# Linear attention: the second half of the scores goes from PSUM to SBUF by ScalarE and is masked there by GpSimd

## The chip, the cores and the metric

The kernel is one program on 1 core of one Trainium2 chip. The metric is the device time of one execution in microseconds (us). The profile is of one execution; its times and its rows are on the same core.

## What is computed

A decoder of two layers over x (64 batches of 128 tokens by 128 channels, f32): linear attention, cross attention, a local transformer of depth two, a Mamba block, cross attention to the context, and a mixture of experts. The change touches the first of these, linear attention with 16 heads of 8 channels, for each batch:

```
q, k, v = split(layernorm(x) @ Wqkv + bqkv)           # heads of 8
feat(t) = exp(clip(unit(t) @ omega * sqrt(2s) - s, -20, 20)) * weight   # 64 features a head
scores  = feat(k) @ feat(q)^T, with zero where the key is later than the query
out     = (scores^T @ v) / max(scores^T @ 1, 1e-6)
x       = x + out @ Wout + bout
```

The reference sums the keys up chunk by chunk; masked scores over the 128 tokens give the same. The mask is a triangle of ones and zeros (`g.tri`, 128x128) by which the scores of every head are multiplied.

## The kernel before

`linear_attention` runs the 64 batches through a pipeline of seven places, NORM, QKV, KEY, FEAT, SCORE, OUT and LAST, numbered 0 to 6. Step n of the pipeline works on batch n at NORM, on batch n - 1 at QKV and so on, so one step holds a piece of each of up to seven batches. `pipeline` writes the first 8 steps out, then runs a loop whose body is 4 steps (14 turns), then 8 more steps in which the batches run out. Every engine has its own `step` function, whose order is written by hand, and executes its instructions strictly in that order. Engines wait for one another by counting semaphores: `Stage.at(name, b)` is the count at which an operation on batch b is done, and `ago=1` or `ago=2` means the batch one or two before, used where a buffer has to be free again.

The scores of one batch are computed in two halves of 8 heads, both into the same PSUM tensor `score` (128 x 1024 f32). The second half's matmuls (`scores(b, 1)`, L432) can start only when the first half was read out. The masked scores stand in SBUF as `sm` (128 x 2 x 1024), one buffer for even and one for odd batches.

In one step, in this order:

- **TensorE:** the features `feat` of FEAT (L449); the second half of the scores of SCORE (L432); the product of masked scores and values of OUT (L469); the q, k, v matmul of QKV (L477); the last projection of LAST (L485); the transposes of the attention output `oT` (L492) and of q and k (L501); the first half of the scores of FEAT (L432); the transpose of `att` (L515); and last the transpose of the normed x of NORM, `xn` (L522), which waits for GpSimd.
- **VectorE:** the mask of the first half (L555), the statistics of the norm (L563 to L566), the mask of the second half (L570), two clips of the exponentials (L579), the bias of q, k, v (L587), the residual (L593), the division by the denominator (L599, L601, L604), the sums of squares (L611, L614).
- **ScalarE:** L373 and L375 (the length of q and k), two exponentials (L382), the copy of `oT` out of PSUM (L388), L393 and L395 (`rstd` of the norm), the squares (L399), and the copies `qkT` (L404), `attT` (L409) and `xnT` (L414).
- **GpSimd:** q and k times their inverse length (L335), the values (L339), then for NORM x minus its mean (L346), that times `rstd` (L350, gives `xn`) and x plus bias (L352).
- **SyncE** loads x.

A matmul group that waits holds up what stands behind it on TensorE. The three waits of interest are those of L469 (`vec_mask1`, the second mask of its batch), of the first half of the scores (`vec_mask1` of the batch before, which frees `score`) and of L522 (`pool_norm`).

Of the kernel before, what the change touches and what calls it, by code (L numbers as in the profile page):

```python
# [13 lines left out]
T = 128  # L14
# [210 lines left out]
def linear_attention(nc, g):  # L225
# [8 lines left out]
    with ExitStack() as stack:  # L234
# [29 lines left out]
        vec_qkv = Stage(m.sem("vec_qkv"), "qkv ss ssm")  # L264
        vec_mask1 = Stage(m.sem("vec_mask1"), "m1")
        vec_feat = Stage(m.sem("vec_feat"), "clip0 clip1")
# [27 lines left out]
        with nc.Block() as block:  # L294
# [19 lines left out]
            def _(gp):  # L314
# [6 lines left out]
                for i in range(4):  # L321
                    gp.memset(by_head(vpad[i])[:, :, :, HD:HD + 1], 1.0).then_inc(zeroed, 1)
                for stage in (pool_norm, pool_key):
                    stage.start(gp)
# [4 lines left out]
                def step(at):  # L329
                    b = at(KEY)  # L330
                    if b:
                        l = b.lane
                        qk = qkv[l][:, 0:2 * C].rearrange("p (h e) -> p h e", e=HD)
                        gp.wait_ge(*act_key.at("rn", b))
                        gp.tensor_tensor(qk, qk, ss[l][:, 2].unsqueeze(2).to_broadcast([T, 2 * H, HD]), ALU.mult  # L335
                                         ).then_inc(*pool_key.did("qkn"))
                        gp.wait_ge(*pe_out.at("pv", b, ago=4))
                        split = lambda ap: ap.rearrange("p (j k e) -> p j k e", k=2, e=HD)
                        gp.tensor_tensor(by_head(vpad[b.slot])[:, :, :, 0:HD], split(qkv[l][:, 2 * C:3 * C]),  # L339
                                         split(g.ones[:]), ALU.mult  # L340
                                         ).then_inc(*pool_key.did("v"))
                    b = at(NORM)
                    if b:
# [14 lines left out]
            def _(sc):  # L358
# [4 lines left out]
                sc.activation(fbias[:, 1:2], fbias[:, 0:1], ACT.Ln).then_inc(prep, 1)  # L363
                for stage in (act_norm, act_turn, act_qkv, act_key, act_keyT, act_feat, act_out, act_att):
                    stage.start(sc)
                sc.wait_ge(prep, 8)

                def step(at):
# [16 lines left out]
                    if b:  # L385
                        sc.wait_ge(*pe_out.at("pv", b))
                        sc.wait_ge(*pe_out.at("pvT", b, ago=2))
                        sc.activation(two(oT[b.lane][:]), feat[:, 0, 0:2 * T], ACT.Copy).then_inc(*act_out.did("oT"))  # L388
                    b = at(NORM)
                    if b:  # L390
# [28 lines left out]
            def _(te):  # L419
# [16 lines left out]
                def step(at):  # L436
# [22 lines left out]
                    if b:  # L459
                        te.wait_ge(*vec_mask1.at("m1", b))  # L460
                        te.wait_ge(*pool_key.at("v", b))
# [42 lines left out]
                    if b:  # L504
                        te.wait_ge(*vec_feat.at("clip0", b))
                        te.wait_ge(*vec_mask1.at("m1", b, ago=1))
                        scores(b, 0).then_inc(*pe_score.did("s0"))
# [19 lines left out]
            def _(v):  # L527
# [16 lines left out]
                mm.then_inc(prep, 1)  # L544
                for stage in (vec_norm, vec_qkv, vec_mask1, vec_feat, vec_mask, vec_out, vec_last):
                    stage.start(v)
# [3 lines left out]
                def step(at):  # L550
# [9 lines left out]
                    if b:  # L560
# [5 lines left out]
                        v.bn_aggr(mv[l][:], stats[l][:]).then_inc(*vec_norm.did("mv"))  # L566
                    b = at(SCORE)
                    if b:
                        v.wait_ge(*pe_score1.at("s1", b))
                        v.tensor_tensor(sm[b.lane][:, 1].rearrange("p a i h t -> p (a i h) t"),  # L570
                                        score[:].rearrange("p a i t -> p (a i) t"),
                                        g.tri[:].unsqueeze(1).to_broadcast([T, 8, T]), ALU.mult
                                        ).then_inc(*vec_mask1.did("m1"))
                    b = at(FEAT)
# [2175 lines left out]
```

## Time and profile before

| what | us |
|---|---|
| median of 3 runs | 4103.48 |
| lowest and highest run | 4102.70, 4106.04 |
| span of the profiled execution | 4103.4 |
| linear attention in it, to the start of the next part | 0 to about 490 |
| TensorE busy, of the whole span | 3856.4 (94%) |
| VectorE busy | 3013.6 (73%) |
| ScalarE busy | 2823.1 (69%) |
| GpSimd busy | 1820.6 (44%) |

The profile gives no time of its own for the execution beside the span; the span lies within the three runs, 0.1 us from their median. PE is TensorE's matmuls, PEld its weight loads, DVE VectorE, ACT ScalarE, POOL GpSimd, SP SyncE. The shares are averages over eight parts of the program with different limits; linear attention is about an eighth of the time.

### The profile page before, as it was taken

How to read it: one execution, taken by the hardware profiler on the slowest of the kernel's cores; microseconds unless marked ns; L12 is line 12 of the kernel's file. 1: busy time of each engine (PE TensorE's matmuls, PEld its weight loads, DVE VectorE, ACT ScalarE, POOL GpSimd, SP SyncE). 2: the span in 40 equal slices, each digit the busy share in tenths (PEclk: the TensorE clock that was granted, in tenths of full speed). 3: DMA queues.
4: the chain of work that ended last, by engine and by line, in shares of the span. 5: the costliest groups of instructions: out<-in, count | busy, mean ns of one | idle time of the engine just before them, and what ended most of it. 6: DMA issues, size and time to landing. Idle time of an engine off the chain costs nothing. (4 is left out here: it accounts for less than half of the span.)

```text
span 4103.4 us, 106549 instructions
## 1 busy us (share of the span) xinstructions
PE 3856.4 (94%) x33992; PEld 2993.1 (73%) x33992; DVE 3013.6 (73%) x7587; ACT 2823.1 (69%) x6420; POOL 1820.6 (44%) x1728
## 2 busy tenths in 40 slices
PE   7888899999979999898999989999999989998999
PEld 5666688888746666685666677888888867776777
DVE  7888655555569999657999955777777767775665
ACT  5666455555569999757999975777777767774333
POOL 3333222222258888536777753333333321112443
PEclk9999999999999999999999999999999989999999
DMA  0000100000010000100000010000000000000000
GB/s 18 9 9 10 48 8 6 6 6 6 7 43 9 8 8 8 27 18 10 8 8 8 13 28 29 1 0 0 0 0 0 0 3 4 3 3 6 12 12 12
DMA packets 109259, 42.48 MB, mean 10 GB/s; under 512 B 91232, under 2 KB 107872, under 8 KB 108512
## 3 DMA queue, kind: packets, MB, share of 16 engines
q1 hardware_dynamic: 109152, 41.10, 3.9%
q8 instruction: 61, 1.00, 0.1%
q14 instruction: 46, 0.38, 0.0%
HBM read 20.16 MB, written 4.19 MB: 6 GB/s over the span
## 5 line engine op out<-in xcount | busy, mean ns | idle before, releaser
L1142 POOL TENSOR_TENSOR l_rc<-l_rc,l_rs 128x1024 f32<-128x1024 f32 x128 | 303.6, 2372 | 201.4 <-DVE l_rs L1334 201.4
L1209 ACT ACTIVATE l_prob<-l_prob,l_mx 128x128 f32<-128x128 f32 x1024 | 312.1, 390 | 0.0
L1820 POOL TENSOR_TENSOR mb_steps<-w_upto,mb_dta 128x1024 f32<-128x1024 f32 x64 | 121.4, 1896 | 354.7 <-DVE mb_dta L2077 354.7
L711 POOL TENSOR_TENSOR ca_prob<-ca_prob,ca_sm 128x1232 f32<-128x1232 f32 x64 | 143.9, 2249 | 299.3 <-DVE ca_sm L877 299.3
L1234 PE MATMUL l_qk_ps<-w_local,l_hT 128*128 128x512 f32 x512 | 248.8, 609 | 13.1 <-DVE l_rs L1334 11.1
L1136 POOL TENSOR_TENSOR l_prob<-l_prob,l_sm 128x1024 f32<-128x1024 f32 x128 | 242.8, 1897 | 16.9 <-DVE l_sm L1320 16.9
L1119 POOL TENSOR_TENSOR l_rc<-l_rc,l_ss 128x1024 f32<-128x1024 f32 x128 | 243.4, 1902 | 12.5 <-POOL l_rc L1142 4.5
L1977 PE MATMUL mb_x_ps<-w_wx,mb_xT 128*128 128x256 f32 x1024 | 236.9, 384 | 0.0
L1329 DVE TENSOR_REDUCE l_ss<-l_sq 128x16 f32<-128x1024 f32 x128 | 156.1, 1219 | 77.3 <-ACT l_sq L1173 76.9
L2542 POOL TENSOR_TENSOR mo_hid<-mo_hid,mo_gate 128x1024 f32<-128x1024 f32 x64 | 121.7, 1901 | 201.7 <-DVE mo_hid L2688 201.7
L1977 PEld LDWEIGHTS mb_x_ps<-w_wx,mb_xT 128*128 128x128 f32 x1024 | 190.0, 191 | 23.2
L1242 PEld LDWEIGHTS l_att_ps<-l_probT,l_val 128*64 128x64 f32 x2048 | 109.2, 136 | 128.3 <-ACT l_probT L1160 128.3
L738 ACT ACTIVATE ca_oT<-ca_go_ps 128x1024 f32<-128x1024 f32 x64 | 65.5, 1024 | 190.2 <-PE ca_go_ps L791 190.2
L2027 DVE SCALAR_TENSOR_TENSOR mb_pre<-mb_bc_ps,w_steps,mb_pre 128x127 f32<-128x127 f32 (+2 forms) x576 | 192.8, 342 | 1.7 <-ACT mb_pre L1868 1.6
L1484 PE MATMUL m_ag_ps<-m_hT,w_gated 128*128 128x256 f32 (+1 forms) x768 | 181.2, 387 | 1.8 <-DVE m_hT L1567 1.8
L2244 POOL TENSOR_TENSOR xa_kblock<-xa_kT,xa_gmask 128x308 f32<-128x308 f32 x64 | 44.8, 700 | 283.8 <-ACT xa_kT L2284 283.8
L1271 PEld LDWEIGHTS l_score_ps<-l_kT,l_qT 64*128 64x128 f32 x2048 | 124.2, 187 | 63.5 <-issue 50.8
L2265 ACT ACTIVATE xa_probT<-xa_prob_ps 77x1024 f32<-77x1024 f32 x128 | 130.5, 1020 | 55.4 <-PE xa_prob_ps L2316 55.4
L2573 ACT ACTIVATE mo_hidT<-mo_turn_ps 128x512 f32<-128x512 f32 x128 | 69.5, 595 | 141.4 <-PE mo_turn_ps L2617 141.4
L1242 PE MATMUL l_att_ps<-l_probT,l_val 128*64 128x128 f32 x2048 | 140.1, 279 | 27.0 <-ACT l_probT L1160 10.3
L1298 DVE TENSOR_TENSOR l_prob<-l_score_ps,k_local 128x1024 f32<-128x1024 f32 x128 | 155.7, 1216 | 13.1 <-PE l_score_ps L1271 9.4
L1317 DVE TENSOR_REDUCE l_sm<-l_prob 128x8 f32<-128x1024 f32 x128 | 155.4, 1214 | 8.6 <-ACT l_prob L1209 4.6
(354 smaller groups left out, 11993.2 us busy)
## 6 DMA issues: line engine op xcount, KB each, us to landing
la_xin<-in_x SPq DMA_DIRECT2D x64, 64.0 KB
l_h<-lt_y SPq DMA_DIRECT2D x128, 32.0 KB
lt_quad<-lt_y SPq DMA_DIRECT2D x32, 128.0 KB
out_x<-k_x SPq DMA_DIRECT2D x64, 64.0 KB, 1.5
l_h<-lt_y SPq DMA_DIRECT2D x128, 31.8 KB
lt_quad<-lt_y SPq DMA_DIRECT2D x32, 127.0 KB
ca_ctxT<-in_ctx_T SPq DMA_DIRECT2D x128, 19.2 KB
wr_state<-in_p_state SPq DMA_DIRECT2D x1, 2438.5 KB, 11.9
```

Source lines behind the costliest of these rows:

```text
L1119: gp.tensor_tensor(rc[l][:].rearrange("p a h e -> p (a h) e"), rc[l][:].rearrange("p a h e -> p (a h) e"), ss[l][:, 2].unsqueeze(2).to_bro ...
L1136: gp.tensor_tensor(heads, heads, sm[b.lane][:, 1].unsqueeze(2).to_broadcast([T, H, T]), ALU.mult).then_inc(*pool_prob.did("norm"))
L1142: gp.tensor_tensor(wide(rc[l][:]), wide(rc[l][:]), wide(rs[l][:]), ALU.add).then_inc(*pool_sum.did("rot"))
L1209: ex = sc.activation(p[:, a, j], p[:, a, j], ACT.Exp, bias=mx[l][:, a, j:j + 1])
L1234: mm = te.matmul(qk_ps[:, a], hT[b.slot][:], wqkv[:, a], start=True, stop=True)
L1242: mm = te.matmul(att_ps[HD * a:HD * a + HD, j], val[b.slot][:, 2 * j + a], probT[l][:, a, j], start=True, stop=True)
L1298: v.tensor_tensor(prob[b.slot][:].rearrange("p a j t -> p (a j) t"), score_ps[:].rearrange("p a j t -> p (a j) t"), g.local[:].unsqueeze(1 ...
L1317: v.tensor_reduce(sm[l][:, 0], prob[b.slot][:].rearrange("p a j t -> p (a j) t"), AX, ALU.add).then_inc(*vec_sum.did("sum"))
L1329: v.tensor_reduce(ss[l][:, 0], sq[l][:].rearrange("p a h e -> p (a h) e"), AX, ALU.add).then_inc(*vec_rot.did("ss"))
L1484: mm = te.matmul(ag_ps[half][0:M[c], c, N * a:N * a + N], w1[:, a, 128 * c:128 * c + M[c]], hT[b.lane][:, N * half:N * half + N], start=Tr ...
L1977: mm = te.matmul(x_ps[:, DI * k:DI * k + DI], xT[l][:, at_j:at_j + T], wx[:, k, j], start=(j == 0), stop=(j == TAPS - 1))
L2027: v.scalar_tensor_tensor(out=out, in0=bc_ps[:, T * i + there.start:T * i + there.stop], scalar=cw[:, k, 2 + SHIFTED[i][1], TAPS - 1 - back ...
```

## The change

For the second half of the scores VectorE's mask L570 is gone. In its place ScalarE copies the whole half (128 x 1024 f32) from PSUM to `sm`, behind the copy of `oT` and ahead of `rstd`. GpSimd then multiplies it in place by the triangle, behind the values and ahead of NORM's operations. TensorE's product of scores and values waits for GpSimd (`pool_mask`), and its next first half of the scores, which reuses the PSUM, waits for ScalarE's copy (`act_score`).

```diff
--- before.py
+++ after.py
@@ -262,7 +262,8 @@
         x_in = m.lanes("x_in")
         vec_norm = Stage(m.sem("vec_norm"), "stats mv")
         vec_qkv = Stage(m.sem("vec_qkv"), "qkv ss ssm")
-        vec_mask1 = Stage(m.sem("vec_mask1"), "m1")
+        act_score = Stage(m.sem("act_score"), "s1")
+        pool_mask = Stage(m.sem("pool_mask"), "m1")
         vec_feat = Stage(m.sem("vec_feat"), "clip0 clip1")
         vec_mask = Stage(m.sem("vec_mask"), "m0")
         vec_out = Stage(m.sem("vec_out"), "den rden att")
@@ -320,7 +321,7 @@
                 gp.wait_ge(zeroed, NZERO)
                 for i in range(4):
                     gp.memset(by_head(vpad[i])[:, :, :, HD:HD + 1], 1.0).then_inc(zeroed, 1)
-                for stage in (pool_norm, pool_key):
+                for stage in (pool_norm, pool_key, pool_mask):
                     stage.start(gp)
                 gp.wait_ge(loaded, NLOAD)
                 gp.wait_ge(made, NMADE)
@@ -339,6 +340,12 @@
                         gp.tensor_tensor(by_head(vpad[b.slot])[:, :, :, 0:HD], split(qkv[l][:, 2 * C:3 * C]),
                                          split(g.ones[:]), ALU.mult
                                          ).then_inc(*pool_key.did("v"))
+                    b = at(SCORE)
+                    if b:
+                        heads = sm[b.lane][:, 1].rearrange("p a i h t -> p (a i h) t")
+                        gp.wait_ge(*act_score.at("s1", b))
+                        gp.tensor_tensor(heads, heads, g.tri[:].unsqueeze(1).to_broadcast([T, 8, T]), ALU.mult
+                                         ).then_inc(*pool_mask.did("m1"))
                     b = at(NORM)
                     if b:
                         l = b.lane
@@ -361,7 +368,8 @@
                 sc.activation(fweight[:, 1:2], fweight[:, 0:1], ACT.Sqrt).then_inc(prep, 1)
                 sc.preload_act_table_set("natural_log_exp_and_others")
                 sc.activation(fbias[:, 1:2], fbias[:, 0:1], ACT.Ln).then_inc(prep, 1)
-                for stage in (act_norm, act_turn, act_qkv, act_key, act_keyT, act_feat, act_out, act_att):
+                for stage in (act_norm, act_turn, act_qkv, act_key, act_keyT, act_feat, act_out, act_att,
+                              act_score):
                     stage.start(sc)
                 sc.wait_ge(prep, 8)
 
@@ -386,6 +394,13 @@
                         sc.wait_ge(*pe_out.at("pv", b))
                         sc.wait_ge(*pe_out.at("pvT", b, ago=2))
                         sc.activation(two(oT[b.lane][:]), feat[:, 0, 0:2 * T], ACT.Copy).then_inc(*act_out.did("oT"))
+                    b = at(SCORE)
+                    if b:
+                        sc.wait_ge(*pe_score1.at("s1", b))
+                        sc.wait_ge(*pe_out.at("pv", b, ago=2))
+                        sc.activation(sm[b.lane][:, 1].rearrange("p a i h t -> p a (i h t)"),
+                                      score[:].rearrange("p a i t -> p a (i t)"), ACT.Copy
+                                      ).then_inc(*act_score.did("s1"))
                     b = at(NORM)
                     if b:
                         l = b.lane
@@ -457,7 +472,7 @@
                         scores(b, 1).then_inc(*pe_score1.did("s1"))
                     b = at(OUT)
                     if b:
-                        te.wait_ge(*vec_mask1.at("m1", b))
+                        te.wait_ge(*pool_mask.at("m1", b))
                         te.wait_ge(*pool_key.at("v", b))
                         te.wait_ge(*act_out.at("oT", b, ago=1))
                         if at(FEAT):
@@ -503,7 +518,7 @@
                     b = at(FEAT)
                     if b:
                         te.wait_ge(*vec_feat.at("clip0", b))
-                        te.wait_ge(*vec_mask1.at("m1", b, ago=1))
+                        te.wait_ge(*act_score.at("s1", b, ago=1))
                         scores(b, 0).then_inc(*pe_score.did("s0"))
                     b = at(OUT)
                     if b:
@@ -542,7 +557,7 @@
                     for a in (0, 1):
                         mm = v.tensor_tensor(omega[:, q, a], omega[:, q, a], scale, ALU.mult)
                 mm.then_inc(prep, 1)
-                for stage in (vec_norm, vec_qkv, vec_mask1, vec_feat, vec_mask, vec_out, vec_last):
+                for stage in (vec_norm, vec_qkv, vec_feat, vec_mask, vec_out, vec_last):
                     stage.start(v)
                 v.wait_ge(prep, 8)
                 v.wait_ge(made, NMADE)
@@ -564,13 +579,6 @@
                         v.wait_ge(*vec_norm.at("stats", b))
                         v.memset(rstd[l][:, 1:2], 0.0)
                         v.bn_aggr(mv[l][:], stats[l][:]).then_inc(*vec_norm.did("mv"))
-                    b = at(SCORE)
-                    if b:
-                        v.wait_ge(*pe_score1.at("s1", b))
-                        v.tensor_tensor(sm[b.lane][:, 1].rearrange("p a i h t -> p (a i h) t"),
-                                        score[:].rearrange("p a i t -> p (a i) t"),
-                                        g.tri[:].unsqueeze(1).to_broadcast([T, 8, T]), ALU.mult
-                                        ).then_inc(*vec_mask1.did("m1"))
                     b = at(FEAT)
                     if b:
                         for u in (0, 1):
```

The order on GpSimd, in the loop's body: one step of the pipeline from the q and k scaling to the bias of x. `la_qkv` and `la_ss` are KEY's, `la_sm` is SCORE's, `la_off` and `la_xn` are NORM's. Before:

```order
L335 TENSOR_TENSOR la_qkv<-la_qkv,la_ss 128x256 [waits la_act_key]
L337 REGISTER_ALU
L339 TENSOR_TENSOR la_vpad<-la_qkv,k_ones 128x16x8 [waits la_pe_out]
L345 REGISTER_ALU
L346 TENSOR_TENSOR la_off<-la_xin,la_mv 128x128 [waits la_act_norm]
L348 REGISTER_ALU
L349 REGISTER_ALU [waits la_pool_norm]
L350 TENSOR_TENSOR la_xn<-la_off,la_rstd 128x128 [waits la_pe_norm]
```

and with the change (the lines of the file have moved by one to seven):

```order
L336 TENSOR_TENSOR la_qkv<-la_qkv,la_ss 128x256 [waits la_act_key]
L338 REGISTER_ALU
L340 TENSOR_TENSOR la_vpad<-la_qkv,k_ones 128x16x8 [waits la_pe_out]
L347 TENSOR_TENSOR la_sm<-la_sm,k_tri 128x1024 [waits la_act_score]
L352 REGISTER_ALU
L353 TENSOR_TENSOR la_off<-la_xin,la_mv 128x128 [waits la_act_norm]
L355 REGISTER_ALU
L356 REGISTER_ALU [waits la_pool_norm]
L357 TENSOR_TENSOR la_xn<-la_off,la_rstd 128x128 [waits la_pe_norm]
```

The multiplication of `la_sm` by `k_tri` stands between KEY's and NORM's operations, with a wait on ScalarE's copy.

The order on ScalarE, in the same step: from the copy of `oT` to `rstd`. Before:

```order
L388 ACTIVATE la_oT<-la_feat 128x256 [waits la_pe_out]
L392 REGISTER_ALU
L393 ACTIVATE la_rstd<-la_mv,la_eps 128x1 [waits la_vec_norm]
L394 REGISTER_ALU
L395 ACTIVATE la_rstd<-la_rstd 128x1 [waits la_act_norm]
```

and with the change:

```order
L396 ACTIVATE la_oT<-la_feat 128x256 [waits la_pe_out]
L399 REGISTER_ALU
L400 REGISTER_ALU [waits la_pe_score1]
L401 ACTIVATE la_sm<-la_score 128x1024 [waits la_pe_out]
L407 REGISTER_ALU
L408 ACTIVATE la_rstd<-la_mv,la_eps 128x1 [waits la_vec_norm]
L409 REGISTER_ALU
L410 ACTIVATE la_rstd<-la_rstd 128x1 [waits la_act_norm]
```

The copy of the scores stands between `oT` and the two operations of `rstd`.

## Rows read from the trace of the kernel before

**Rows 1.** Busy time of each engine in two stretches of linear attention, with granted clock

```profile
core 0: us, PE busy (x) PEld busy (x) DVE busy (x) ACT busy (x) POOL busy (x), PEclk, DMA share, GB/s
24.92:39.12 14.20, 10.88 (x142) 7.98 (x142) 11.61 (x26) 8.26 (x20) 5.61 (x10) 1.00 0.04 12
100.00:129.00 29.00, 26.01 (x368) 19.38 (x362) 23.93 (x57) 18.24 (x45) 10.29 (x20) 1.00 0.03 9
```

**Rows 2.** Timeline of one step, VectorE: start us, duration us, engine, line, operation, operands

```profile
213.04 1.22 DVE L555 TENSOR_TENSOR la_sm<-la_score,k_tri 128x1024 f32<-128x1024 f32 x1
...
215.61 1.23 DVE L570 TENSOR_TENSOR la_sm<-la_score,k_tri 128x1024 f32<-128x1024 f32 x1 [0.93 <-PE la_score L432]
...
216.75 1.53 DVE L579 TENSOR_SCALAR la_ef<-la_ef,la_high,la_low 128x1024 f32<-128x1024 f32 x2
```

**Rows 3.** Timeline of the same step, TensorE, ScalarE and GpSimd; idle before in brackets

```profile
213.17 1.15 PE L449 MATMUL la_feat<-la_qkT,la_w 32*128 32x256 f32 x16
...
216.86 0.38 ACT L388 ACTIVATE la_oT<-la_feat 128x256 f32<-128x256 f32 x1 [0.35 <-PE la_feat L469]
...
217.14 0.29 ACT L393 ACTIVATE la_rstd<-la_mv,la_eps 128x1 f32<-128x1 f32 x1
...
217.46 0.20 ACT L395 ACTIVATE la_rstd<-la_rstd 128x1 f32<-128x1 f32 x1
...
217.74 0.80 POOL L346 TENSOR_TENSOR la_off<-la_xin,la_mv 128x128 f32<-128x128 f32 x1 [2.59 <-ACT la_rstd L395]
...
218.15 1.16 PE L432 MATMUL la_score<-la_ef 64*128 64x128 f32 x16
...
218.69 0.40 POOL L350 TENSOR_TENSOR la_xn<-la_off,la_rstd 128x128 f32<-128x128 f32 x1 [0.16 <-POOL la_off L346]
...
219.78 0.33 PE L515 MATMUL la_turned<-k_ident,la_att 128*128 128x128 f32 x1 [0.46 <-DVE la_att L604]
...
220.06 0.32 PE L522 MATMUL la_front<-k_ident,la_xn 128*128 128x128 f32 x1
...
220.31 1.15 PE L449 MATMUL la_feat<-la_qkT,la_w 32*128 32x256 f32 x16
```

**Rows 4.** Timeline, the first matmul group behind the loop's turn

```profile
228.11 1.15 PE L449 MATMUL la_feat<-la_qkT,la_w 32*128 32x256 f32 x16 [0.55 <-issue]
```

**Rows 5.** Groups of instructions: busy us, mean ns of one, idle before

```profile
L738 ACT ACTIVATE ca_oT<-ca_go_ps 128x1024 f32<-128x1024 f32 x64 | 65.5, 1024 | 190.2 <-PE ca_go_ps L791 190.2
```

**Rows 6.** Timeline of the kernel's start, GpSimd and TensorE

```profile
17.22 0.40 POOL L346 TENSOR_TENSOR la_off<-la_xin,la_mv 128x128 f32<-128x128 f32 x1
...
17.70 0.40 POOL L350 TENSOR_TENSOR la_xn<-la_off,la_rstd 128x128 f32<-128x128 f32 x1
...
18.15 0.47 PE L522 MATMUL la_front<-k_ident,la_xn 128*128 128x128 f32 x1 [0.56 <-POOL la_xn L350]
...
18.55 2.09 PE L449 MATMUL la_feat<-la_qkT,la_w 32*128 32x256 f32 x16
```

**Rows 7.** Groups of instructions on GpSimd, whole span

```profile
L1142 POOL TENSOR_TENSOR l_rc<-l_rc,l_rs 128x1024 f32<-128x1024 f32 x128 | 303.6, 2372 | 201.4 <-DVE l_rs L1334 201.4
...
L1136 POOL TENSOR_TENSOR l_prob<-l_prob,l_sm 128x1024 f32<-128x1024 f32 x128 | 242.8, 1897 | 16.9 <-DVE l_sm L1320 16.9
...
L352 POOL TENSOR_TENSOR k_x<-la_xin,la_w 128x128 f32 x56 | 25.4, 453 | 0.0
L2249 POOL TENSOR_TENSOR k_x<-k_x,wl_context 128x128 f32 x56 | 22.9, 409 | 27.0 <-DVE xa_xn L2454 27.0
...
L1430 POOL TENSOR_TENSOR lt_y<-lt_y,w_gated 128x512 f32 x16 | 17.5, 1092 | 0.0
```

**Rows 8.** Timeline of the end of linear attention, ScalarE and TensorE

```profile
482.80 0.38 ACT L388 ACTIVATE la_oT<-la_feat 128x256 f32<-128x256 f32 x1 [2.82 <-PE la_feat L469]
...
484.82 1.08 PE L469 MATMUL la_feat<-la_sm,la_vpad 128*32 128x128 f32 x32
```

## The prediction

> **What bounds the kernel now.** The change lies in the first stage, linear attention, so I read that stage alone. The table of busy time by stretch [rows 1] shows TensorE busy 90% there (26.01 of 29 us), VectorE 83% and GpSimd 35%, at granted clock 1.00. No engine is full; the stage is a loop of waits. The timeline of one ordinary step shows which. On VectorE [rows 2] the first mask starts at 213.04, the second (L570) at 215.61 after 0.93 us idle for the second scores, the two clips at 216.75; from there VectorE runs without a gap to the next first mask. On TensorE [rows 3] the features matmul (L449) starts at 213.17 and again at 220.31: a step is 7.14 us. The transpose of the attention output (L515) waits 0.46 us for VectorE. So today's limit is VectorE: mask, scores, mask, clips, the small operations behind them, next mask. Every fourth step is the loop's turn and longer: the next features matmul comes at 228.11, 7.80 us after 220.31, with 0.55 of issue in front of it [rows 4].
>
> **What the change removes.** The second mask, 1.23 us of VectorE per step, and the 0.93 us in front of it. VectorE then only waits for the exponentials before its clips. That alone would leave TensorE's own row as the floor: 7.14 less the 0.46 it waits at L515 and what small waits it has elsewhere, some 6.5 us.
>
> **What it adds, and where it stands.** ScalarE's copy stands behind the copy L388 (oT), which waits for the product L469, which waits for the exponential L382, which waits for the features matmul. GpSimd's mask stands behind that copy and, in GpSimd's order, ahead of the norm's two operations (L346, then L350). L350 makes what TensorE transposes last in its step (L522), and the next features matmul stands behind that transpose. That closes a loop that has to be gone round once per step. I walk it from the features matmul at 0:
>
> - to the start of ScalarE's operation behind oT: 217.14 - 213.17 = 3.97 [rows 3]. The new copy takes this place; its scores have been ready since about 2.4.
> - the copy: 1.02, from a 128x1024 f32 Copy out of PSUM [rows 5]. It ends at 4.99.
> - ScalarE to GpSimd: 0.08 (L395 ends 217.66, L346 starts 217.74 [rows 3]). 5.07.
> - the mask: priced below, 2.37. 7.44.
> - L346 and L350 behind it: 0.40, 0.08 between, 0.40, as they run at the start of the kernel [rows 6]. 8.32.
> - to TensorE's transpose 0.05 (18.10 to 18.15 [rows 6]), and from there to the next features matmul 0.25 (220.06 to 220.31 [rows 3]). 8.62, or some 8.60.
>
> In today's step L346 takes 0.80, not 0.40, and ends 0.26 after the clips end (218.54 against 218.28) [rows 2, 3]. GpSimd stands still while VectorE's clips run. In the new order the clips lie at about 2.3 to 4.2 and the mask at 5.1 to 7.4, so I add nothing. The Trainium skill (SBUF — State Buffer, "SBUF: two separate sides") calls this an exclusive lock on a port pair that the two engines share; the rows agree. By that rule VectorE's small SBUF operation L614 would wait for the mask, and the first mask with it to about 7.7. It would still end at 8.9, before TensorE can use it at 8.6 + 1.24 = 9.8, so the sum stays.
>
> **The price of the mask.** No row has this operation. GpSimd's 128x1024 multiplications with one value held per run of elements take 1.90; with two operands that both change at every element 2.37 [rows 7]. The triangle is repeated over the 8 heads, but both operands change at every element. There is a row of that very shape, L1430 (four blocks by one row, 512 elements, 1.09), which would scale to about 2.0. Small ones split too: 0.453 (L352) and 0.409 (L2249) for the same 128x128 sum. In the program's memory layout, the dear ones have both operands at the same place within 16 bytes, the cheap ones do not; the scores and the triangle do. Hence 2.37, with 1.90 as the lower end. No row suggests less than 1.90. A page has a price as well: the Trainium skill (GPSIMD Engine Reference, "Performance versus the Vector engine") gives 4497 ns for 2048 elements, by which I estimate 2.25 for 1024, and the end would be about 4185; no run here shows that operation.
>
> **The sum.** 8.60 against 7.14 is +1.46 per step. The turn's extra time stays in the loop as before. The mask and the norm are both in a step for batches 4 to 63 of the pipeline's count, 60 steps; in the last ones there is no norm, and the loop does not exist. 60 x 1.46 = 88. At the end of the stage the last L469 waits for the mask: oT starts at 482.80, so 482.80 + 0.28 + 1.02 + 0.08 + 2.37 = 486.55 against 484.82 today [rows 8], +1.7. The first of the 60 has no oT and is about 0.6 cheaper. Together +89. Everything else has one answer: TensorE's wait for the scores' PSUM (L432, first half) is now for ScalarE's copy, ended at 4.99, where TensorE arrives at 4.98 (218.15 - 213.17 [rows 3]), so it costs 0.1 to 0.2 us that the wait for the norm hides; ScalarE has 18.24 / 29 x 7.14 = 4.5 us of work per step [rows 1], then 5.5 of 8.6; no DMA is touched, and xin's load is two steps ahead. The profiled execution's span is 4103.4 us, and the median of the runs 4103.48, so both give **4192 us**.
>
> **The rivals.**
> - *The mask is cheap* (1.90 to 2.06): the same loop at 8.13 to 8.3, 60 x 0.99 + 1.3 = +61 to +71, 4164 to 4174. For it speaks L1430.
> - *GpSimd is held up further*: if VectorE's small operations in the mask's time stop it as the clips stop L346, some 0.4 us per step, +24, 4216. Against it: L350 keeps its 0.40 at 218.69 [rows 3], where VectorE is in the middle of them without a gap.
> - *TensorE's clock falls*. TensorE now pauses some 1.8 us per step; its busy share falls to about 6.5 of 8.6, 76%. At the half level (1.2 GHz, the first matmuls) the features matmul takes 2.09 instead of 1.15 [rows 6, 3]; with a like loss at L469 the loop grows by 1 to 2 us, +60 to +120, about 4280. Against it: between 24.92 and 39.12 TensorE was busy 10.88 of 14.20, 77%, at clock 1.00 [rows 1].
> - *Faster*: VectorE's relief shows. The loop through GpSimd without the mask is 8.60 - 2.37 = 6.23, so the mask must take under 0.91 us for a step to be shorter than 7.14; at 0.3 or less the step is TensorE's 6.5 and the time 4103 - 60 x 0.64 = 4065. The one thing for it is that spans on GpSimd are rough; against it stands every 1024-element row.
> - *No difference*: the mask near 0.9, or a norm that is not as urgent as I read it. Then 4103.
>
> **Chances.** Forecast (mask about 2.2 to 2.4) 0.60, cheap mask 0.24, held up further 0.06, clock 0.04, faster 0.03, no difference 0.03. Within 0.2% is within 8 us, about what a measurement tells from no change. Slower by more: 0.94. The range reaches from just under the cheap mask, 4160, to the held-up case, 4216; it leaves out the clock, no difference and faster, one in ten.
>
> **What would show it.** Right: GpSimd's mask at about 2.37 us, idle before it on ScalarE's copy; L346's successor starting the moment the mask ends and at 0.40; TensorE idle about 1.8 us per step before the transpose of the norm, released by GpSimd; features matmuls 8.6 us apart; VectorE with long idle time. Wrong: TensorE waiting last for VectorE, or a mask under 1 us, or a transpose that finds its input ready.

## The result and the profile after

| what | before | after |
|---|---|---|
| median | 4103.09 us of 4 runs (4102.64 to 4106.04) | 4275.89 us of 4 runs (4274.67 to 4278.95) |
| ratio, with its 95% interval | | 1.042 (1.0407 to 1.0432) |
| span of the profiled execution | 4103.4 us | 4273.4 us |
| mean granted TensorE clock over the span | 0.983 | 0.961 |
| TensorE, VectorE, ScalarE, GpSimd busy | 3856.4, 3013.6, 2823.1, 1820.6 us | 3941.3, 3006.2, 2878.3, 1950.6 us |

The kernel is 173 us slower. The forecast was 89 us slower, and 4276 lies outside the range of 4160 to 4216. (A fourth run of the kernel before came in with those of the changed one, hence its median of 4103.09 beside the 4103.48 known ahead.)

First the loop, since it is what the forecast was made of. This is the timeline of one step of the changed kernel, from one features matmul to the transpose that frees the next, lines of the other work left out (columns as in [rows 2, 3]: start, duration, engine, line, operation, idle before):

```profile
214.05 1.15 PE L464 MATMUL la_feat<-la_qkT,la_w 32*128 32x256 f32 x16
...
217.74 0.38 ACT L396 ACTIVATE la_oT<-la_feat 128x256 f32<-128x256 f32 x1 [0.35 <-PE la_feat L484]
218.02 1.02 ACT L401 ACTIVATE la_sm<-la_score 128x1024 f32<-128x1024 f32 x1
...
219.12 2.35 POOL L347 TENSOR_TENSOR la_sm<-la_sm,k_tri 128x1024 f32<-128x1024 f32 x1 [3.08 <-ACT la_sm L401]
...
220.28 0.33 PE L530 MATMUL la_turned<-k_ident,la_att 128*128 128x128 f32 x1
...
220.39 1.12 DVE L622 TENSOR_SCALAR la_ss<-la_ss 128x32 f32<-128x32 f32 x1
...
221.42 1.21 DVE L570 TENSOR_TENSOR la_sm<-la_score,k_tri 128x1024 f32<-128x1024 f32 x1
221.42 0.40 POOL L353 TENSOR_TENSOR la_off<-la_xin,la_mv 128x128 f32<-128x128 f32 x1
221.98 0.40 POOL L357 TENSOR_TENSOR la_xn<-la_off,la_rstd 128x128 f32<-128x128 f32 x1 [0.16 <-POOL la_off L353]
...
222.51 0.32 PE L537 MATMUL la_front<-k_ident,la_xn 128*128 128x128 f32 x1 [1.90 <-POOL la_xn L357]
223.39 2.09 PE L464 MATMUL la_feat<-la_qkT,la_w 32*128 32x256 f32 x16 [0.56 <-issue]
225.41 2.08 PE L447 MATMUL la_score<-la_ef 64*128 64x128 f32 x16
```

Counted from the features matmul at 214.05: the copy starts at 3.97, the mask at 5.07, the norm's second operation (L357) ends at 8.33, and the transpose L537 starts at 8.46. The walk of the prediction had 3.97, 5.07, 8.32 and 8.37. TensorE waits 1.90 us for GpSimd there. The step is the one that the forecast described.

The last two lines are what it did not have. After its pause the features matmul runs 2.09 us and not 1.15, and the scores behind it 2.08 and not 1.16: TensorE is at the lower of its two clock levels, 1.2 GHz instead of 2.4. How often that is, shows in the busy time by stretch of the changed kernel (columns as in [rows 1]):

```profile
24.92:39.12 14.20, 11.16 (x120) 8.16 (x119) 8.53 (x17) 7.97 (x17) 5.61 (x8) 0.76 0.04 12
100.00:129.00 29.00, 22.52 (x253) 16.69 (x254) 16.16 (x34) 14.99 (x32) 12.40 (x18) 0.82 0.02 7
100.00:450.00 350.00, 274.64 (x3127) 206.37 (x3128) 204.05 (x449) 187.10 (x415) 158.52 (x210) 0.84 0.02 7
```

Before, both short stretches had clock 1.00 [rows 1]. Now the clock is 0.76 and 0.82, and 0.84 over 350 us of the stage. In the groups of instructions between 60 and 500 us each of the three large matmul groups has a longer mean (busy us, mean ns of one, idle before):

```profile
L447 PE MATMUL la_score<-la_ef 64*128 64x128 f32 x1392 | 133.6, 346 | 3.7
...
L464 PE MATMUL la_feat<-la_qkT,la_w 32*128 32x256 f32 x704 | 68.4, 516 | 5.7 <-issue 5.7
L484 PE MATMUL la_feat<-la_sm,la_vpad 128*32 128x128 f32 x1408 | 61.5, 330 | 1.2 <-ACT la_ef L390 1.2
...
L622 DVE TENSOR_SCALAR la_ss<-la_ss 128x32 f32<-128x32 f32 x44 | 45.9, 1043 | 1.5
...
L537 PE MATMUL la_front<-k_ident,la_xn 128*128 128x128 f32 x44 | 14.6, 331 | 83.3 <-POOL la_xn L357 83.3
```

The same three groups of the kernel before, in the same stretch:

```profile
L432 PE MATMUL la_score<-la_ef 64*128 64x128 f32 x1872 | 136.0, 284 | 3.7 <-DVE la_sm L555 1.2
...
L449 PE MATMUL la_feat<-la_qkT,la_w 32*128 32x256 f32 x928 | 66.5, 400 | 7.3 <-issue 7.2
...
L469 PE MATMUL la_feat<-la_sm,la_vpad 128*32 128x128 f32 x1920 | 64.9, 275 | 8.2 <-ACT la_ef L382 6.1
```

Per step (16 features matmuls, 32 for the scores, 32 for the product) the busy time is 3.07 us instead of 2.32 for the scores, 1.55 instead of 1.15 for the features and 1.40 instead of 1.08 for the product, together 1.47 us more. The step above is 8.71 us with the clock up (the transpose at 8.46, and 0.25 to the next features matmul); 223.39 stands at the loop's turn and so comes 0.6 later. The masks run from 29.3 to 652.2 us, 63 steps apart, 9.89 us a step on average, the turns among them.

TensorE's pause before the transpose is 83.3 us in 44 waits, 1.89 us each. And L622, VectorE's small operation that was 0.18 us before, takes 1.04: it stands still until the mask ends, as the timeline shows (220.39 + 1.12 is 221.51, the mask ends at 221.47).

### The profile page after: what moved, and what is told of

Same layout as the page of the kernel before. It is cut to its first block and busy times, and to the rows that moved or that the text cites. A ratio compares the mean times of both kernels' runs of the same rounds, so it can differ in the third digit from the quotient of the medians.

```text
span 4273.4 us, 106706 instructions
## 1 busy us (share of the span) xinstructions
PE 3941.3 (92%) x33992; PEld 3058.4 (72%) x33992; DVE 3006.2 (70%) x7523; ACT 2878.3 (67%) x6484; POOL 1950.6 (46%) x1792
## 5 line engine op out<-in xcount | busy, mean ns | idle before, releaser
L347 POOL TENSOR_TENSOR la_sm<-la_sm,k_tri 128x1024 f32<-128x1024 f32 x64 | 150.5, 2351 | 275.8 <-ACT la_sm L401 275.8
L587 DVE TENSOR_SCALAR la_ef<-la_ef,la_high,la_low 128x1024 f32<-128x1024 f32 x128 | 104.1, 813 | 175.2 <-ACT la_ef L390 175.2
L447 PEld LDWEIGHTS la_score<-la_ef 64*128 64x128 f32 x2048 | 166.9, 241 | 55.4 <-issue 53.3
L447 PE MATMUL la_score<-la_ef 64*128 64x128 f32 x2048 | 193.9, 343 | 9.4 <-DVE la_sm L570 2.6
L390 ACT ACTIVATE la_ef<-la_feat,la_fbias 128x1024 f32<-128x1024 f32 x128 | 135.7, 1111 | 53.5 <-PE la_feat L464 53.5
```

Of the source, the lines that this page charges most:

```text
L347: gp.tensor_tensor(heads, heads, g.tri[:].unsqueeze(1).to_broadcast([T, 8, T]), ALU.mult).then_inc(*pool_mask.did("m1"))
L447: mm = te.matmul(score[:, a, 2 * i2 + half], ef[b.lane][rows, 2 * u + i2, half, 1], ef[b.lane][rows, 2 * u + i2, half, 0], start=True, sto ...
```

## The experiments

Two theories stood at the start. Theory 1: the loop through copy, mask and norm costs what the forecast said, and TensorE's lower clock, brought on by the pause, costs the rest. The rival: the whole 173 us come from the loop and from waits that the walk has missed, and the lower clock only goes along with it and costs nothing.

### filler: TensorE kept busy in its pause

Eight needless products of the identity by itself, written to a place that the transpose overwrites, ahead of the wait for the norm:

```diff
                     if b:
-                        te.wait_ge(*pool_norm.at("xn", b))
                         te.wait_ge(*act_turn.at("xnT", b, ago=1))
                         if at(QKV):
                             te.wait_ge(*vec_qkv.at("qkv", at(QKV)))
+                        for _ in range(8 if at(OUT) else 0):
+                            te.matmul(front[:, 3 * C:4 * C], g.ident[:], g.ident[:], start=True, stop=True)
+                        te.wait_ge(*pool_norm.at("xn", b))
                         te.transpose(front[:, 3 * C:4 * C], xn[b.lane][:], g.ident[:]).then_inc(*pe_norm.did("xnT"))
```

> The change, with eight needless 128x128 matmuls of the identity per step on TensorE in the pause in which it waits for GpSimd's norm (about 1.9 us; eight of them take about 8 x 0.22 = 1.76 us at full clock). Theory 1 (two causes: the longer loop through GpSimd, and on top of it TensorE at its half clock level for part of each step, because of that pause): the granted clock goes back to about 1.0, steps are 8.71 us as the undisturbed one of the changed kernel, mean 8.87 with the loop's turn, against 9.88 now; 4103 + 60 x (8.87 - 7.27) + 2 = about 4200. Theory 2 (the clock is a symptom, the loop alone sets the time): no gain, 4275, or more for the added work.

Measured: 4200.48 us (4197.6 to 4201.71), ratio 1.0235 (1.0217 to 1.0252). The timeline of one step, TensorE alone:

```profile
217.32 1.15 PE L464 MATMUL la_feat<-la_qkT,la_w 32*128 32x256 f32 x16
...
223.54 0.33 PE L530 MATMUL la_turned<-k_ident,la_att 128*128 128x128 f32 x1
...
223.71 1.95 PE L537 MATMUL la_front<-k_ident 128*128 128x128 f32 x16
...
225.71 0.33 PE L539 MATMUL la_front<-k_ident,la_xn 128*128 128x128 f32 x1
...
225.97 0.71 PE L464 MATMUL la_feat<-la_qkT,la_w 32*128 32x256 f32 x8
```

The busy time between 100 and 450 us:

```profile
100.00:450.00 350.00, 330.43 (x4228) 265.39 (x4224) 233.76 (x516) 214.40 (x476) 182.10 (x240) 1.00 0.03 7
```

(One needless product shows as two matmuls in these lines: x16 for eight.) The clock is 1.00 and the step 8.65 us (217.32 to 225.97). The kernel does more work and is 75 us faster. So the loop has 2.35%, about 96 us of the 173, and the clock has the other 76. Nearly all of that lies between the first and the last mask: filler's start at 28.4 and 576.8 us, 8.70 us a step with the turns, where the changed kernel has 9.89, which is 74.5 us over the 63 steps. The rival falls.

### fill4, lump, lump1, split, split1: what in the pause the clock goes by

My reading after the first runs was that the length of one pause decides. fill4 is filler with 4 products in place of 8; lump has 2 and lump1 has 1, all at the start of the pause. In split and split1 the same 2 or 1 stand in its middle:

```diff
+                        if at(SCORE):
+                            te.wait_ge(*pool_mask.at("m1", at(SCORE)))
+                            for _ in range(2):
+                                te.matmul(front[:, 3 * C:4 * C], g.ident[:], g.ident[:], start=True, stop=True)
+                        te.wait_ge(*pool_norm.at("xn", b))
```

> As filler, with four needless matmuls instead of eight: TensorE's pause before the norm's transpose is about 1.0 us where the change has 1.9 and eight matmuls left none. Theory 1 (a pause of about 1 us is short enough, as in the kernel before at its start, 77% busy at clock 1.00): clock 1.0, steps of 8.65 us, 4200. Theory 2 (the clock falls in proportion to the idle time): about halfway, 4235.

> Separates the length of TensorE's pause from its busy share. In the pause before the transpose of the norm TensorE now waits first for GpSimd's mask, does two needless 128x128 products there (about 0.25 us), then waits for the norm. The pause of about 1.8 us becomes two of some 0.8 to 0.9 us; the work per step grows by two small products only. If the length of a single pause decides, the granted clock between 100 and 450 us is 0.98 to 1.00 and the time 4200 to 4210. If TensorE's busy share decides (81% here, as in the run with the moved triangle, whose clock was 0.86), the clock is 0.84 to 0.88 and the time 4250 to 4275.

> The same two needless products, at the start of the pause instead of in its middle: one pause of about 1.65 us. Both theories expect a clock of 0.84 to 0.88 and 4245 to 4275; it is the comparison for the run in which the pause is split.

> The run with two needless products at the start of the pause kept its clock (0.98, pause 1.36 us), so it could not serve as comparison. Now one product in place of two, in the middle of the pause, behind the wait for the mask: pauses of about 0.99 and 0.45 us in one step, the same work as in lump1. If the length of a single pause decides: clock 0.98 to 1.00, 4200 to 4212. If the busy share decides: as lump1.

> One needless product at the start of the pause: one pause of about 1.62 us, between the run with the moved triangle (1.55 us, clock 0.86) and the changed kernel (1.9 us, clock 0.84). Both theories expect the clock lost, 0.84 to 0.90, and 4240 to 4275. If the clock is kept here too, the pause alone does not order the runs.

| kernel | needless products | TensorE's pauses, an ordinary step | clock, 100 to 450 us | median us | ratio (95%) |
|---|---|---|---|---|---|
| after | 0 | 1.90 | 0.84 | 4275.89 | 1.042 (1.0407 to 1.0432) |
| lump1 | 1, at the start | 1.61 | 0.86 | 4258.98 | 1.0378 (1.0361 to 1.0396) |
| split1 | 1, in the middle | 1.01 and 0.37 | 0.86 | 4261.08 | 1.0384 (1.0367 to 1.0402) |
| lump | 2, at the start | 1.39 | 0.98 | 4212.55 | 1.0269 (1.0251 to 1.0286) |
| split | 2, in the middle | 1.01 and 0.14 | 0.98 | 4209.80 | 1.0263 (1.0246 to 1.028) |
| fill4 | 4, at the start | 0.94 | 0.99 | 4205.73 | 1.0254 (1.0238 to 1.027) |
| filler | 8, at the start | none | 1.00 | 4200.48 | 1.0235 (1.0217 to 1.0252) |

A step of split1, TensorE's timeline:

```profile
215.49 0.33 PE L530 MATMUL la_turned<-k_ident,la_att 128*128 128x128 f32 x1
216.82 0.46 PE L539 MATMUL la_front<-k_ident 128*128 128x128 f32 x2 [1.01 <-DVE la_ss L626]
217.65 0.33 PE L541 MATMUL la_front<-k_ident,la_xn 128*128 128x128 f32 x1 [0.36 <-POOL la_xn L357]
218.50 1.51 PE L464 MATMUL la_feat<-la_qkT,la_w 32*128 32x256 f32 x16 [0.52 <-issue]
219.93 2.08 PE L447 MATMUL la_score<-la_ef 64*128 64x128 f32 x16
```

and one of lump:

```profile
218.10 0.61 PE L538 MATMUL la_front<-k_ident 128*128 128x128 f32 x4
220.10 0.33 PE L540 MATMUL la_front<-k_ident,la_xn 128*128 128x128 f32 x1 [1.39 <-POOL la_xn L357]
220.36 1.15 PE L464 MATMUL la_feat<-la_qkT,la_w 32*128 32x256 f32 x16
```

The features matmuls at 218.50 in split1 and at 223.39 in the changed kernel stand at the loop's turn, with 0.52 and 0.56 us of issue on top of the pause; the table's pauses are those of steps without a turn. The changed kernel has the lower level in steps without a turn as well: its features matmul of the step at 243.25 us takes 2.09.

(The releaser of the first pause in split1 is printed as VectorE's L626. The wait in the code is for GpSimd's mask, and L626 is held until that mask ends, so the two end together.)

The expectations of fill4 (clock 1.0, 4200, against 4235 by the idle time) and of split (0.98 to 1.00, 4200 to 4210) came out near my reading, but that of lump did not: 0.84 to 0.88 and 4245 to 4275 were expected, 0.98 and 4212.55 measured. The other theory, TensorE's busy share, had been put down for split with the same 0.84 to 0.88 and missed there and in lump. The last pair, split1 and lump1, decided against my reading, which had 0.98 to 1.00 and 4200 to 4212 for split1; it came out as lump1, as the busy share had it there. No pause of an ordinary step of split1 is longer than 1.01 us, and its clock is 0.86, that of lump1 with its 1.61; lump keeps 0.98 with a pause of 1.39. Cutting the pause in two changed nothing, in both pairs. One more product per step, of about 0.22 us, was worth 46 us (4258.98 to 4212.55) at one place and 51 at the other. So the length of one pause does not sort these runs, and what the chip goes by stays open; they only tell which kernels kept the clock, and what it cost those that did not.

### offset: is the mask dear because of where its operands lie?

The prediction chose 2.37 us for the mask because both operands start at the same place within 16 bytes. Here GpSimd reads a copy of the triangle, in a buffer of its own, that starts 8 bytes off:

```diff
+        tri2 = m.sb("tri2", [128, T + 4])
...
-                gp.wait_ge(zeroed, NZERO + 4)
+                gp.tensor_tensor(tri2[:, 2:2 + T], g.tri[:], g.ones[:], ALU.mult).then_inc(zeroed, 1)
+                gp.wait_ge(zeroed, NZERO + 5)
...
-                        gp.tensor_tensor(heads, heads, g.tri[:].unsqueeze(1).to_broadcast([T, 8, T]), ALU.mult
+                        gp.tensor_tensor(heads, heads, tri2[:, 2:2 + T].unsqueeze(1).to_broadcast([T, 8, T]), ALU.mult
```

> The change, with a second copy of the triangle that begins 8 bytes off the 16-byte grid on which the scores begin, used by GpSimd's mask alone. Theory 1 (the place of the two operands within 16 bytes sets the price): the mask takes about 2.0 us instead of 2.35; steps shorter by 0.35 at least, so about 4250, less if the shorter pause also keeps more of the clock. Theory 2 (the price is that of two operands that both change at every element): 2.35 us and 4275 as now.

Measured: 4238.16 us (4235.2 to 4244.35), ratio 1.0325 (1.0308 to 1.0342). The mask in its timeline, and the transposes' pause:

```profile
217.77 2.00 POOL L349 TENSOR_TENSOR la_sm<-la_sm,la_tri 128x1024 f32<-128x1024 f32 x1 [4.74 <-ACT la_sm L403]
...
220.82 0.33 PE L539 MATMUL la_front<-k_ident,la_xn 128*128 128x128 f32 x1 [1.54 <-POOL la_xn L359]
```

The same multiplication takes 2.00 us and not 2.35, with nothing changed but where one operand lies. That it is the 8 bytes, and not the other buffer as such, fits the prediction's reading of [rows 7], but has no run of its own: a copy of the triangle with an aligned start was not tried. TensorE's pause shrinks by as much, 1.90 to 1.54. And the busy time of this kernel at the kernel's start and in the stage:

```profile
24.92:39.12 14.20, 10.61 (x140) 7.71 (x137) 10.46 (x22) 10.04 (x21) 7.18 (x9) 1.00 0.05 12
100.00:450.00 350.00, 282.60 (x3314) 212.40 (x3316) 204.46 (x481) 198.54 (x443) 154.64 (x220) 0.86 0.02 7
```

Between 24.92 and 39.12 us TensorE is busy 75% at clock 1.00, and then the stage has 0.86. That is the very stretch which the prediction used, in the kernel before, against a fall of the clock. It tells nothing about the stage. split1 has 1.00 there as well, and 0.86 in the stage.

### half: a mask of half the size

GpSimd masks 4 of the 8 heads and leaves the other 4 unmasked:

```diff
-                        heads = sm[b.lane][:, 1].rearrange("p a i h t -> p (a i h) t")
+                        heads = sm[b.lane][:, 1, 0].rearrange("p i h t -> p (i h) t")
...
-                        gp.tensor_tensor(heads, heads, g.tri[:].unsqueeze(1).to_broadcast([T, 8, T]), ALU.mult
+                        gp.tensor_tensor(heads, heads, g.tri[:].unsqueeze(1).to_broadcast([T, 4, T]), ALU.mult
```

> The change with GpSimd masking only half of what it copies (4 of 8 heads, 512 elements; the other 4 stay unmasked). Mask 1.27 us instead of 2.35 (the 512-element row of the kernel before). Theory 1 (loop through GpSimd, clock kept where the pause is short): step 8.65 - 1.08 = 7.57, pause 0.8 us, clock 1.0, 4103 + 60 x 0.46 + 1 = about 4132. Theory 2 (the clock falls as soon as the loop is GpSimd's, whatever the pause): 4160 or more.

Measured: 4140.17 us (4135.95 to 4145.16), ratio 1.0096 (1.0081 to 1.0112). Its timeline:

```profile
223.97 1.27 POOL L347 TENSOR_TENSOR la_sm<-la_sm,k_tri 128x512 f32<-128x512 f32 x1 [3.11 <-ACT la_sm L401]
...
226.29 0.32 PE L537 MATMUL la_front<-k_ident,la_xn 128*128 128x128 f32 x1 [0.82 <-POOL la_xn L357]
```

The mask is 1.08 us shorter than the 2.35 of the changed kernel, and the transpose comes 7.65 us after the one before it (218.64 to 226.29), where it was 8.71: the mask stands on the loop at its full length. The clock is 0.99. Against filler's 4200.48 that is 60 us less, 1.0 us for each of the 60 steps.

### nomask and swap: what the relief of VectorE is worth, and the order on GpSimd

nomask has no mask on GpSimd at all, and TensorE's product waits for ScalarE's copy; the second half stays unmasked:

```diff
-                    b = at(SCORE)
-                    if b:
-                        heads = sm[b.lane][:, 1].rearrange("p a i h t -> p (a i h) t")
-                        gp.wait_ge(*act_score.at("s1", b))
-                        gp.tensor_tensor(heads, heads, g.tri[:].unsqueeze(1).to_broadcast([T, 8, T]), ALU.mult
-                                         ).then_inc(*pool_mask.did("m1"))
...
-                        te.wait_ge(*pool_mask.at("m1", b))
+                        te.wait_ge(*act_score.at("s1", b))
```

swap computes everything. Its six lines of the mask are those of the changed kernel, moved behind NORM's three operations on GpSimd:

```diff
                         gp.tensor_tensor(flat(g.x[:, bass.ds(b.index, 1), :]), xin[l][:], bout, ALU.add
                                          ).then_inc(*pool_norm.did("xb"))
+                    b = at(SCORE)
+                    if b:
+                        heads = sm[b.lane][:, 1].rearrange("p a i h t -> p (a i h) t")
+                        gp.wait_ge(*act_score.at("s1", b))
+                        gp.tensor_tensor(heads, heads, g.tri[:].unsqueeze(1).to_broadcast([T, 8, T]), ALU.mult
+                                         ).then_inc(*pool_mask.did("m1"))
```

> The change without GpSimd's mask (the second half of the scores is left unmasked); TensorE's product waits for ScalarE's copy instead. This shows what freeing VectorE is worth when nothing takes its place. Theory 1: TensorE's first half of the scores waits for the copy and its own row sets the step, 6.8 us, so 4103 - 60 x 0.35 = about 4082, clock 1.0. Theory 2 (the copy on ScalarE is itself a loss): 4103 or more.

> The change, with GpSimd's mask behind the norm's three operations of the same step, where it stood ahead of them. Theory 1 (what costs is that the norm is queued behind the mask): TensorE gets the norm at about 6.5 us of the step, the mask runs 6.9 to 9.2, that is until 2.4 of the next step, just before TensorE needs it at 2.5; steps of 6.8 to 7.1 us, clock 1.0, time 4083 to 4100. Theory 2 (GpSimd's work as such is too much, or it and VectorE's clips hold each other up when the mask reaches into the time of the clips): the q and k scaling comes late, steps of 7.5 us or more, 4125 or more.

Measured: nomask 4084.32 us (4084.14 to 4086.09), ratio 0.9952 (0.9936 to 0.9969); swap 4090.7 us (4087.46 to 4092.71, 7 runs), ratio 0.9969 (0.9958 to 0.998). A step of swap, GpSimd and TensorE:

```profile
218.49 1.15 PE L464 MATMUL la_feat<-la_qkT,la_w 32*128 32x256 f32 x16 [0.55 <-issue]
...
223.96 0.40 POOL L347 TENSOR_TENSOR la_off<-la_xin,la_mv 128x128 f32<-128x128 f32 x1 [2.75 <-ACT la_rstd L410]
...
224.53 0.40 POOL L351 TENSOR_TENSOR la_xn<-la_off,la_rstd 128x128 f32<-128x128 f32 x1 [0.17 <-POOL la_off L347]
...
225.06 0.32 PE L537 MATMUL la_front<-k_ident,la_xn 128*128 128x128 f32 x1
...
225.30 2.36 POOL L359 TENSOR_TENSOR la_sm<-la_sm,k_tri 128x1024 f32<-128x1024 f32 x1
225.31 1.15 PE L464 MATMUL la_feat<-la_qkT,la_w 32*128 32x256 f32 x16
```

The norm is ready before TensorE comes for it, the transpose L537 waits for nothing, the clock between 100 and 450 us is 1.00, and the step is 6.82 us. The mask now runs beside the features and scores matmuls, and those that need it (L484) come only after both. How much they wait for it, the tile's own view tells (who waited for the mask; us, times):

```profile
L359 POOL TENSOR_TENSOR la_sm<-la_sm,k_tri x64: 2342/2361/2374, 30.8 to 466.3; 128x1024 f32<-128x1024 f32 x64
...
  PE la_feat L484: 5.4, 17
```

The same 2.36 us of mask, one place later in GpSimd's queue, hold up TensorE by 5.4 us in all. nomask, with no mask at all, is another 6 us ahead of swap, and is my measure of the most that relieving VectorE is worth: 0.3 to 0.6%, some 20 us. swap gets about 13 of them. Its whole interval lies below the kernel before, by 0.2 to 0.4%; of the versions that compute everything, only swap and the next one, swapoff, are faster than both kernels.

### swapoff: both together

swap with the moved triangle of offset.

> swap and offset together: the mask behind the norm and at 2.0 us. Theory 1: in swap the mask ended just at the time TensorE and the first clip wanted it (TensorE waited for it in 14 of 44 steps); 0.35 us less takes that wait away, so 4084 to 4090, near the kernel without any mask on GpSimd. Theory 2 (nothing left to gain there): 4091 as swap.

Measured: 4089.0 us (4087.8 to 4091.71, 6 runs), ratio 0.9969 (0.9957 to 0.9981). With the shorter mask (2.00 us) the time can't be told from that of swap. TensorE's wait for the mask, 5.4 us in 17 times in swap, is down to 1.3 us in one, so there was little left to gain.

### spare: GpSimd's work without the wait

The kernel before, VectorE still masking both halves, with a 128x1024 multiplication by the triangle on a buffer of its own in the place where the changed kernel has its mask. Nothing waits for its result, and it waits for no other engine:

```diff
+                    b = at(SCORE)
+                    if b:
+                        gp.wait_ge(*pool_idle.at("i", b, ago=1))
+                        gp.tensor_tensor(idle[:, 1], idle[:, 0], g.tri[:].unsqueeze(1).to_broadcast([T, 8, T]), ALU.mult
+                                         ).then_inc(*pool_idle.did("i"))
```

> The kernel before, with a needless GpSimd multiplication of 128x1024 by the triangle (a buffer of its own) in the place where the change has its mask, but waiting for nothing: it runs from about 2.0 to 4.3 us of the step, when GpSimd is idle, and ends before the norm's operations could start. Theory 1 (the change costs because the mask waits for the copy and the norm stands behind it, not because of GpSimd's work): no delay of the norm; what is left is that VectorE's first clip waits for it, 0.6 to 0.7 us per step, so about 4145. Theory 2 (2.35 us more work on GpSimd cost as such): 4190 or more. Theory 3 (GpSimd and VectorE do not hold each other up): 4103.

Measured: 4146.54 us (4145.73 to 4152.9), ratio 1.0107 (1.0092 to 1.0123). Its timeline:

```profile
219.02 1.74 DVE L587 TENSOR_SCALAR la_ef<-la_ef,la_high,la_low 128x1024 f32<-128x1024 f32 x2
...
220.15 0.86 POOL L354 TENSOR_TENSOR la_off<-la_xin,la_mv 128x128 f32<-128x128 f32 x1 [0.67 <-ACT la_rstd L403]
...
224.88 2.38 POOL L348 TENSOR_TENSOR la_idle<-la_idle,k_tri 128x1024 f32<-128x1024 f32 x1
...
226.38 1.43 DVE L587 TENSOR_SCALAR la_ef<-la_ef,la_high,la_low 128x1024 f32<-128x1024 f32 x1
```

Work that nobody waits for costs 44 us here. The clip that meets it takes 1.43 us, and over the stretch from 100 to 450 us the clips' mean is 1.05 where it was 0.81. (The norm's L354 behind the clips takes 0.86; that is not new, in the kernel before it took 0.80 [rows 3].) VectorE was the bound of that kernel, so what holds up its clips holds up the step: 128 clips, each 0.24 us longer, are 31 us by my estimate. The clock, at 0.97 between 100 and 450 us, has a part in the 44 us that I did not separate. In the changed kernel the clips are done before the mask begins, and only the small L622 meets it.

## Why the prediction was wrong, point by point

- **What bounds the kernel before, and the relief.** VectorE was the bound. But what can be had by relieving it is small: TensorE's own floor, put at 6.5 us, shows as 6.82 in swap and nomask, and the faster of these is at 4084 where the rival "faster" had 4065.
- **The walk round the loop: right.** Copy at 3.97, mask at 5.07, norm finished at 8.33 against 8.32. The transpose came 0.13 us behind it, not 0.05, so a step is 8.71 (8.65 in filler), not 8.60. The wait between L353 and L357 was 0.16, as in [rows 3], not 0.08 as in [rows 6]; L353 began 0.05 before the mask's end, and the mask was 0.02 shorter, which hid it.
- **The price of the mask: right.** 2.35 us against 2.37. The choice among [rows 7] by the operands' places agrees with offset (2.00), though no run had an aligned copy to compare.
- **L614 (now L622) waits for the mask, and it does not matter: right.** 1.04 us in place of 0.18, and filler's step is no longer for it. The Trainium skill (SBUF — State Buffer, "SBUF: two separate sides") gave this by its exclusive lock; the trace agrees, with L622 ending 0.04 us after the mask.
- **The sum of the loop: +89 against about 96 measured** (filler). The interval of filler's ratio reaches from 89 to 103 us, so the forecast's figure is at its edge. A step of 8.65 instead of 8.60 accounts for 3 us of the 7; the rest I did not trace.
- **The rival "TensorE's clock falls": this is the step that failed.** The sum had TensorE's lower clock at nothing, and it cost 76 us on top of the loop. The rival had its mechanism, its place (the features matmul at 2.09, the product as well) and its price: +60 to +120 against 76 measured. That its 4280 comes so near to 4275.89 is in part luck, as the loop was put 7 us too low and the clock, by its middle, some 12 too high. What failed is the reason for putting the term at nothing, and with it the chance of 0.04 and the exclusion from the range. Both rested on one row, 77% busy at clock 1.00 between 24.92 and 39.12 us [rows 1]. Offset has 75% at clock 1.00 in that stretch and 0.86 in the stage: 14 us at the start do not speak for 450 us of steady steps. Nothing else spoke against it, and [rows 6] showed what it would cost, so in my judgment it deserved a chance near one half, and a range that takes in its 4280.
- **The other rivals.** The mask was not cheap. GpSimd was not held up further: L353 and L357 ran at 0.40 each.

The Trainium skill (TensorE: Matmul & The Clock Gate, "A second HAM failure mode: psum-queue depth-cycling") describes a kernel in which frequent short idle times between matmul groups made the clock alternate between its levels. I did not weigh it in the prediction. The trace agrees with it: TensorE's idle time comes in pauses of 1.9 us, and groups at 1.15 us and at 2.09 us follow one another.

## What to carry to other kernels

Work that is moved to a lightly used engine stands in that engine's queue, and what matters is what is behind it there: put it behind the operation that a busy engine waits for next, as swap did, since the order alone was worth 185 us here, the clock's part included, where the relief itself was worth some 20 at most. Where a change gives TensorE a pause in every step, price its clock as a term of the sum, from the rows at the lower level, and look for the counterargument in a steady stretch with such a step and not in the start of the kernel. A few needless matmuls in such a pause are a cheap test of whether the clock is what is being lost.

## What the runs showed of the hardware that I had not expected

- The loss of TensorE's clock is steep. One needless product less per step (about 0.22 us of 8.65) took the stage from 0.98 to 0.86, and 46 us with it. It did not matter whether the pause was whole (1.61 us) or cut in two (1.01 and 0.37 us).
- The same GpSimd multiplication of 128x1024 takes 2.35 us with both operands at the same place within 16 bytes and 2.00 us with one of them in another buffer and 8 bytes off (after and offset).
- A GpSimd operation that nothing waits for cost the kernel 1.07% (spare). VectorE's clips took 1.05 us on average beside it, where they took 0.81; the granted clock of 0.97 has a part in the cost that was not separated.
